# Attention and FFN block on one core: separate waits for each turned half, each v tile and each half of q and k; scores by precision pass; rk on GpSimd

## The reference

```
xn = (x - mean) / sqrt(var + 1e-5)
q, k, v = xn @ wq, xn @ wk, xn @ wv        # 8 heads of 128
q, k = rope(q), rope(k)
s = q @ k^T / 128, causal mask             # per batch and head, 512 x 512
o = softmax(s) @ v
attn = sum over heads of o @ wo
h = s0 * ([xn, -xn] @ sign(k0)); h = 2 * relu(h)      # 1024 wide
h = s1 * (h @ sign(k1));         h = 2 * relu(h)      # 1024 wide
ffn = s2 * (h @ sign(k2))
out = x + attn + ffn
```

## Time and profile before

| what | us |
|---|---|
| median of 3 runs (1779.66 to 1780.92) | 1779.78 |
| the profiled execution, its own time | 1781.45 |
| its span from first to last instruction | 1779.6 |
| TensorE, VectorE busy in the span | 1723.5, 1535.5 |

### The profile page before, as it was taken

One profiled execution on the slowest core, in us unless ns is written; L12 is line 12 of the kernel. 1 busy time (PEld: TensorE's weight loads), 2 busy tenths in 40 slices (PEclk: granted clock), 3 DMA queues, 4 the chain that ended last, 5 costly groups with the idle time before them and its releaser, 6 DMA issues.

```text
span 1779.6 us, 34027 instructions
## 1 busy us (share of the span) xinstructions
PE 1723.5 (97%) x12720; PEld 1196.4 (67%) x12720; DVE 1535.5 (86%) x3628; ACT 1269.1 (71%) x2715; POOL 923.6 (52%) x952
## 2 busy tenths in 40 slices
PE   6899989999999999999999999999999999999998
PEld 2456757767676676767767677676766767677667
DVE  8899888897988979898897988979889798888974
ACT  6777676777867678676776867778676776767773
POOL 6555544554545555455455545545455554555542
PEclk9999999999999999999999999999999999999999
DMA  5234543344343434334244433443533343343433
GB/s 171 48 55 72 94 68 78 66 82 80 55 96 63 80 66 72 78 66 96 56 87 73 66 78 66 84 78 55 96 66 78 66 72 82 63 95 59 80 65 66
DMA packets 454838, 134.08 MB, mean 75 GB/s; under 512 B 434704, under 2 KB 453648, under 8 KB 454672
## 3 DMA queue, kind: packets, MB, share of 16 engines
q1 hardware_dynamic: 454672, 131.90, 39.8%
HBM read 14.94 MB, written 8.39 MB: 13 GB/s over the span
## 4 chain that ended last, share of the span: by engine, by line
PE 67%; DVE 18%; DMA 4%; ACT 4%; POOL 3%; issue 3%; SPq 0%; DVEq 0%; POOLq 0%
PE bank L484 67%; DMA pt<-ph 3%; DVE ph L696 3%; DVE p L659 2%; DVE bank L618 2%; DVE bank L610 2%; DVE qk L628 2%; ACT p L673 2%; DVE rt L834 1%; DMA xT<-rt 1%; POOL tb L614 1%; POOL xT L316 1%; DVE v L538 1%; DVE hb L815 1%; DVE o L538 1%
## 5 line engine op out<-in xcount | busy, mean ns | idle before, releaser
L690 POOL TENSOR_SCALAR ph<-p,ri 128x384 f16<-128x384 f32 (+3 forms) x512 | 311.7, 609 | 453.5 <-DVE rk L680 416.2
L614 POOL TENSOR_TENSOR tb<-tb,sin 128x512 f32<-128x512 f32 x256 | 331.6, 1296 | 250.8 <-ACT tb L606 245.2
L484 PE MATMUL bank<-hb,wa 128*128 128x256 f16 x3360 | 379.7, 273 | 0.0
L484 PEld LDWEIGHTS bank<-hb,wa 128*128 128x128 fp8e5 x3360 | 328.0, 98 | 41.3
L673 ACT ACTIVATE p<-p,nm,sc 128x512 f32<-128x512 f32 (+3 forms) x512 | 328.6, 645 | 1.6
L696 DVE SCALAR_TENSOR_TENSOR ph<-p,rk,ph 128x512 f16<-128x512 f32 (+3 forms) x512 | 311.8, 616 | 0.0
L659 DVE CUSTOM_DVE_ANT_0 p<-bank,mask 128x512 f32<-128x512 f32 (+3 forms) x512 | 229.2, 485 | 51.1 <-PE bank L484 48.0
L484 PE MATMUL bank<-pt,v 128*128 128x256 f16 (+1 forms) x2304 | 234.0, 256 | 16.1 <-DMA pt<-ph 15.8
L484 PE MATMUL bank<-qk 128*128 128x512 f16 (+3 forms) x1536 | 231.4, 300 | 16.3 <-DVE qk L628 14.0
L484 PEld LDWEIGHTS bank<-pt,v 128*128 128x128 f16 x2304 | 203.3, 98 | 44.3 <-DMA pt<-ph 22.9
L484 PEld LDWEIGHTS bank<-qk 128*128 128x128 f16 x1536 | 133.3, 98 | 123.0 <-DVE qk L628 22.4
(11 more groups left out here) (107 smaller groups left out, 2265.5 us busy)
## 6 DMA issues: line engine op xcount, KB each, us to landing
out<-xnat SPq DMA_DIRECT2D x32, 256.0 KB, 2.3
xnat<-in_x SPq DMA_DIRECT2D x15, 512.0 KB, 3.9
pt<-ph SPq DMA_TRANSPOSE x256, 4.3
o<-in_k SPq DMA_DIRECT2D x1, 1024.0 KB, 7.8
v<-in_wq SPq DMA_DIRECT2D x1, 1024.0 KB, 9.8
v<-in_wk SPq DMA_DIRECT2D x1, 1024.0 KB, 11.6
ph<-in_wv SPq DMA_DIRECT2D x1, 1024.0 KB, 14.0
o<-in_wo SPq DMA_DIRECT2D x1, 1024.0 KB, 10.8
```

The lines of the kernel that those rows point to most:

```text
L484: self.todo.append(lambda e, stop=False: e.matmul(self.ps[:, cols[0]:cols[1]], lhsT, rhs, start=first, stop=stop, skip_group_check=skip))
L614: done["crossed", n] = pool.put(lambda e: e.tensor_tensor(tb, tb, SIN[:], ALU.mult))
L690: done["P_hi", g, i] = pool.put(lambda e: e.tensor_scalar(part(r, i, HI), v, RI[:, g % 4, i:i + 1], 4096.0, ALU.mult, ALU.mult))
```

## The change

- `s_pt` becomes a semaphore for each buffer and each q. `turned(q)` waits only for its own P_lo and issues its own transfer. The one for q = 1 has the due time `turned`, the one for q = 0 the new `turned_0`.
- `high(i)` waits for the transfer of its own q of two heads before. `values` waits, run by run, for the transfer that the run reads and for v's tile j.
- `scores` takes its three banks at once. It runs HI by HI over all four tiles, then q LO by k HI, then q HI by k LO, and waits before each pass for the halves that it reads. The fills end in the last pass.
- RK is computed on GpSimd ahead of the first P_hi, not on VectorE after RI.
- The tables `PLACES`, `SETUP`, `FIRST`, `EARLY`, `DELAY` and `HELD` have other values.

```
-    "v0": ((-3, 5), (-3, 1), (-1, 0), (0, 4)),
-    "v1": ((3, 5), (4, 1), (4, 0), (1, 4)),
+    "v0": ((-3, 5), (-3, 0), (-1, 0), (0, 4)),
+    "v1": ((3, 5), (3, 4), (4, 0), (1, 4)),
...
-FIRST = ("am0", "l1", "p0", "l1", "qk", "qk", "qk", "am2", "l1", "qk", "p2", "l1", "S", "qk", "S", "l1", "qk", "l1",
-         "v", "v", "v", "v")
+FIRST = ("l1", "am0", "p0", "l1", "qk", "qk", "qk", "am2", "qk", "l1", "p2", "l1", "S", "l1", "qk", "S", "v", "qk",
+         "v", "l1", "v", "v")
...
-EARLY = dict(qhi=(24.5, 21.1, 27.7), qlo=(23.9, 22.6, 17.8), bias=(7.0, 7.5, 7.4), exp=(6.1, 0.6, 5.3),
-             inv=(14.8, 0, 11.4), high=(3.5, 14.3, 15.5), low=(20.6, 36.1, 25.0), turned=(47.2, 23.9, 36.4),
-             rotated=(13.8, 15.3, 11.9))
+EARLY = dict(qhi=(24.1, 21.1, 27.7), qlo=(23.9, 21.8, 17.8), bias=(7.0, 8.5, 7.4), exp=(6.1, 0.6, 2.0),
+             inv=(15.6, 11.1, 11.4), high=(4.9, 14.3, 14.5), low=(21.5, 36.1, 25.0), turned=(46.2, 22.9, 30.8),
+             rotated=(13.8, 15.3, 9.8), turned_0=(52.5, 30, 37.2))
...
-DELAY = dict(hi=0, lo=11.3, swap=0, straight=9.6, crossed=0, rotated=15.5, qhi=21.8, qhi_w=0, qlo=19.8, bias=8.1,
-             exp=11.6, exp_i=1.4, differ=4.7, keep_hi=0, keep_lo=17.4, t_hi=10.6, t_lo=18.1, add=7, inv=23.5,
-             high=22.6, high_i=6.1, low=43.7, low_i=8.3, turned=66.6, x_hi=48.8, x_lo=60.5, x_turned=70.7)
+DELAY = dict(hi=0, lo=11.6, swap=0, straight=9.6, crossed=0, rotated=15.5, qhi=21.8, qhi_w=0, qlo=18.7, bias=8.1,
+             exp=11.6, exp_i=1.4, differ=5, keep_hi=0, keep_lo=16.1, t_hi=9.6, t_lo=18.1, add=7.2, inv=23.5, high=26,
+             high_i=7.9, low=43.7, low_i=8.3, turned=67.4, turned_0=76, x_hi=44.2, x_lo=55.9, x_turned=76.8)
...
-HELD = dict(am=0, p2=23.2, T=30.9, qk=30.5, S=8.2, PV=23.0, v=13.7, l0=25.3, l1=18.3, seg=21.5, l2=18.6, proj=8.7)
+HELD = dict(am=0, p2=18.0, T=22.8, qk=28.8, S=6.4, PV=23.7, v=24.5, l0=24.9, l1=18.3, seg=25.1, l2=17.6, proj=1.3)
...
-        s_pt = [sem("s_pt0"), sem("s_pt1")]
+        s_pt = [[sem(f"s_pt{r}{q}") for q in range(2)] for r in range(2)]
...
         def scores(g):
             r = g % 2
-            pe.wait(*[need(("qk_lo", 2 * g + w)) for w in range(2)])
-            for u, tiles in enumerate(S_FILLS):
-                f = Fill(("S", g, u))
-                at_col = 0
-                spans = []
-                for i in tiles:
-                    w = WIDTH[i]
-                    f.group((at_col, at_col + w),
-                            three(lambda s: QK[:, r, s, i * 128:i * 128 + 128], lambda s: QK[:, r, 2 + s, 0:w]))
-                    spans.append((i, at_col))
-                    at_col += w
-                f.end([("max", g, tiles[-1])])
+            fs = [Fill(("S", g, u)) for u in range(3)]
+            for a, c in ((HI, HI), (LO, HI), (HI, LO)):
+                for f, tiles in zip(fs, S_FILLS):
+                    at_col = 0
+                    for i in tiles:
+                        w = WIDTH[i]
+                        f.wait(need(("qk_lo" if a == LO else "qk_hi", 2 * g)),
+                               need(("qk_lo" if c == LO else "qk_hi", 2 * g + 1)))
+                        f.mm((at_col, at_col + w), QK[:, r, a, i * 128:i * 128 + 128], QK[:, r, 2 + c, 0:w],
+                             skip=len(tiles) > 1)
+                        at_col += w
+                    if c == HI:
+                        f.begin()
+                    else:
+                        f.end([("max", g, tiles[-1])])
+            for f, tiles in zip(fs, S_FILLS):
+                spans = [(i, sum(WIDTH[j] for j in tiles[:n])) for n, i in enumerate(tiles)]
...
-                dve.wait(done["inv", g])
-                done["inv_k", g] = dve.put(lambda e: e.tensor_scalar(RK[:, g % 4, :], RI[:, g % 4, :], 4096.0, None,
-                                                                     ALU.mult))
...
             def high(i):
-                pool.wait(need(("inv_k", g)))
+                pool.wait(need(("inv", g)))
+                if i == 3:
+                    done["inv_k", g] = pool.put(lambda e: e.tensor_scalar(RK[:, g % 4, :], RI[:, g % 4, :], 4096.0, None,
+                                                                          ALU.mult))
...
-                    pool.wait(need(("pt", g - 2)))
+                    pool.wait(need(("pt", g - 2, SQUARE[i][0])))
...
             def low(i):
-                dve.wait(need(("P_hi", g, i)))
+                dve.wait(need(("P_hi", g, i)), done["inv_k", g])
...
-            def turned():
-                sp.wait(*[need(("P_lo", g, i)) for i in range(4)], need("pad"))
+            def turned(q):
+                sp.wait(*[need(("P_lo", g, i)) for i in SQUARE if SQUARE[i][0] == q], need("pad"))
...
-                for q in range(2):
-                    a, n = SQ_AT[q], 2 * SQ_SIZE[q]
-                    done["pt", g] = sp.dma(lambda e, a=a, n=n: e.dma_start_transpose(
-                        PT[:, r, a // 128:(a + n) // 128, :], PH[:, r, a:a + n]), s_pt[r], 32 * (g // 2) + 16 * q + 16)
+                a, n = SQ_AT[q], 2 * SQ_SIZE[q]
+                done["pt", g, q] = sp.dma(lambda e: e.dma_start_transpose(
+                    PT[:, r, a // 128:(a + n) // 128, :], PH[:, r, a:a + n]), s_pt[r][q], 16 * (g // 2) + 16)
...
-            at(delay("turned", g), turned)
+            at(delay("turned_0", g), lambda: turned(0))
+            at(delay("turned", g), lambda: turned(1))
...
         def values(g):
-            pe.wait(need(("pt", g)))
-            pe.wait(*[need(("vp", b, h // 4, t, LO)) for t in range(4)])
             f = Fill(("PV", g))
             for j, q, i0, i1 in PV_RUNS:
+                f.wait(need(("pt", g, q)), need(("vp", b, h // 4, j, LO)))
```

More of the change, by code:

```diff
@@ L69 @@
     "l0": ((-2, 4), (0, 2), (0, 5), (1, 1)),
[4 rows of a table removed]
[4 rows of a table added]
     "seg": ((2, 2), (2, 3), (3, 2), (3, 3), (3, 3), (4, 0), (4, 2), (5, 4)),
     "seg_15": ((2, 0), (3, 4), (4, 1), (4, 2), (5, 2), (5, 2), (5, 5), (6, 5)),
-    "l2_0": ((2, 3), (4, 4)),
+    "l2_0": ((2, 3), (3, 3)),
     "l2": ((6, 3), (8, 3)),
-    "l2_15": ((8, 0), (7, 0)),
+    "l2_15": ((8, 0), (7, 3)),
     "proj": ((9, 0), (9, 3)),
 }
-SETUP = dict(v_max=93.8, o_max=60.2, a11=48.4, a12=45.7, a22=74.9, s1a=1.1, s1b=15.8, s2a=4.9, s2b=14.7, s3a=4.9,
-             s3b=1.2, s4a=76.1, s4b=91.9, k2=63.2, x1=129.9, wq1=86.9, wk1=108.5, wq2=90.5, wk2=116.1, wq3=111.9,
-             wk3=131.4, wv0=118.9, wv1=82.5, pads=117.2, ascale=168.2, wo0=147.5, wo1=161.6)
@@ L86 @@
-FIRST = ("am0", "l1", "p0", "l1", "qk", "qk", "qk", "am2", "l1", "qk", "p2", "l1", "S", "qk", "S", "l1", "qk", "l1",
-         "v", "v", "v", "v")
-EARLY = dict(qhi=(24.5, 21.1, 27.7), qlo=(23.9, 22.6, 17.8), bias=(7.0, 7.5, 7.4), exp=(6.1, 0.6, 5.3),
-             inv=(14.8, 0, 11.4), high=(3.5, 14.3, 15.5), low=(20.6, 36.1, 25.0), turned=(47.2, 23.9, 36.4),
-             rotated=(13.8, 15.3, 11.9))
+SETUP = dict(v_max=95.2, o_max=56.7, a11=56.6, a12=48.1, a22=75.7, s1a=1.3, s1b=19, s2a=11.1, s2b=14.9, s3a=1.6,
+             s3b=7.6, s4a=76.5, s4b=103.9, k2=64.5, x1=129.9, wq1=86.5, wk1=108.7, wq2=89.5, wk2=112.1, wq3=109.7,
+             wk3=131.8, wv0=120.9, wv1=79.2, pads=98.6, ascale=169.1, wo0=149.7, wo1=158.1)
```

## The result

The changed kernel takes 1814.63 us in the median (1813.58 to 1815.51, 4 runs) against 1780.26 of the kernel before: the ratio is 1.0197, 95% interval 1.0182 to 1.0211. It is slower by 34 us, where the forecast was 9 us faster. The profiled execution has a span of 1812.6 us.

What follows compares the result with a forecast made beforehand. The prediction took TensorE as the bound, its waits set by VectorE's order. Scores -10.0, start -4.0 and PV +5.0 gave -9.0 us; from the profiled 1781.45, less 1.67 to the median, that made 1770.8 us, range 1764 to 1777.

Steps and rivals of the forecast that it cites:

- a bank's reader in front of the scores: Sign that the forecast is wrong: a new TensorE wait entry over 5 us for a bank's reader before the scores.
- The shifted places and setup times: Tables: the new values move work by at most a slot and change no count; 0, within 3 us either way.
- All three banks are asked for before the first score matmul: Scores: the third bank is asked for 1.2 us earlier than before; costed at nothing, as other releasers' waits are small.
- Rival (b): Scores find low halves ready but wait for three free banks instead, losing the 10.0 us: 1780.8 us; chance 0.15.
- Eight banks with the oldest one taken: Banks: the cover named for asking for all three score banks early, at no cost.
- There is nothing left to wait for: Scores: with low halves waited for one by one, each is ready when needed; 10.0 us gained, or none.
- rival (d): Time gained at the scores is lost at the next PV, whose 20 waits grow by 0.55: 1786.8 us; chance 0.12.
- Start (-4.0): Second head's scores near 57.76 us: an l1 fill between covers the 4.03 us wait; 4.0 us gained, bounds 0 and 5.5.
- That only eats from a later wait: Start: l1 ahead of am0 leaves p0 less cover, but only shortens the later wait for the two largest values.
- Transfers (+0.45 each): PV: the long transposing transfer, issued second, lands 0.1 to 0.65 us later; each of 20 waits grows by 0.45 us.
- -0.2 each: PV: rk moved from VectorE to GpSimd shortens each of 20 PV waits by 0.2 us; VectorE loses 22.9 us.
- rival (c): GpSimd and VectorE hinder each other: each rk holds a P_lo for 0.5 us, PV waits grow: 1784.8 us; chance 0.06.

Runs made afterwards that it cites:

- s_only: The kernel before with the changed scores alone (three banks at once, high halves first, maxima due after the whole set): 1804.0 us, ratio 1.0140.
- s_lazy: s_only, but each of the three banks is asked for just before its first matmul, old tables: 1803.0 us, ratio 1.0138.
- halves: q_long with scores bank after bank, in each HI by HI first, then q's LO, then k's LO, each waited for by itself: 1763.8 us, ratio 0.9907.
- q_long: The kernel before with separate waits for transfers and v tiles, the long transfer first on its own two P_lo: 1772.1 us, ratio 0.9957.
- q_short: The kernel before with separate waits for transfers and v tiles alone, the short transfer first, old tables: 1779.3 us, ratio 1.0000.
- r_only: The kernel before with rk on GpSimd alone: 1778.9 us, ratio 0.9996.

## Why the prediction was wrong

The forecast was 1770.8 us, within 1764 to 1777, and 1814.63 was measured; the rivals, from 1756 to 1786.8, do not reach it either. Of the signs named ahead, the one of a bank's reader in front of the scores came (15.8 us behind L819), and qk L628 stayed at 17.7 us in all, not under 2.

1. **"The shifted places and setup times move work by at most a slot and change no count: 0, within 3 us either way."** This step failed, and it carries most of the error of 44 us: 29 of them, each of the two pieces measured by itself on the changed kernel. One v tile was worth 8 us, since it stood between the norm and the first reader of xT; the prediction looked for a count and not for who needs the time that the tile took. Six due times were worth 21 us. The text read DELAY only for the order of the transfers. The tables without the rest cost 47 us.
2. **"All three banks are asked for before the first score matmul ... I cost it at nothing."** Wrong in size and place. Rival (b) named the resource, at 10 us in front of the scores; s_only shows 34.7 us in front of the k products and v tiles, and s_lazy that asking early is not what costs. "Eight banks with the oldest one taken" was no cover, for the oldest is chosen by planned times. In the changed kernel the new HELD has taken these waits away, and those behind L819 (15.8 us) only take the place of waits for low halves: with the old scores it is as slow.
3. **"There is nothing left to wait for" at the scores (-10.0).** Right as a mechanism: the qk L628 waits in front of the scores fell to 4.0 us in the changed kernel and, kept in one bank, the step is worth 8.3 us (halves against q_long). The time saved was not kept in the changed kernel, as rival (d) feared, though (d)'s price and its way (PV) were wrong: PV waits fell from 15.8 to 12.7 us.
4. **Start (-4.0).** The 4.03 us wait went, but others grew by twice as much: the 9th head's PV comes 4.0 us later, an error of 8 us. "That only eats from a later wait" was wrong: the first power's wait grew from 0.40 to 2.72 us, and the later one for the largest value fell only from 3.72 to 2.88. The second power's wait (1.12 to 5.54 us) was not seen. An l1 fill is 8192 columns and a score set 3840, so it is the work of two such sets and not of five; the cover of over 3 us is right.
5. **Transfers (+0.45 each).** The order of landing was right, the size not: 0 with the old tables, and PV waits of 12.7 us in the changed kernel where about 20 were expected. The term leaned to an issue of 1.84 us, the median over both kinds; a short one in front takes 1.23. At the median both have landed 5.7 us after the first start (q_short), where it was 5.5. That long first would pay was right, and it is what the change leaves out: it took away all 20 PV waits, 0.8 us each on average, for 7.5 us of the kernel.
6. **rk (-0.2 each, rival (c)).** -1 us measured for -4, not clear of noise. VectorE's busy time did not fall by 23 us but rose by 13, and not through rk, which alone lowers it by 14.3 (1521.2 us in r_only). The rule cited there, that a GpSimd instruction and a VectorE one with two SBUF inputs exclude each other (the Trainium skill, SBUF — State Buffer, "SBUF: two separate sides"), fits the rows at 384.01 and 387.98, roughly: the P_lo from 387.98 ends 0.55 us after L614 does, and alone it takes 0.74. It speaks of every GpSimd instruction that reads SBUF, so it should have been held against the due times of DELAY, not against rk alone.

## What to carry to other kernels

Where an order is made from due times, a change of the tables is a change of every engine's queue: cost it by what stands between a producer and its first reader, and by what lands beside what, not by counts. When a step holds its banks longer, the choice of banks has to be set again, and the waits turn up in front of other work. Waiting for operands one by one paid where no more buffers were open for it: here 8 us with one bank, while with two the kernel was 2 to 3 us slower than without, and with three 24 us slower than the kernel before (s_only), under the old HELD each time.

## What the runs showed of the hardware that was not expected

P_lo, with two inputs in SBUF, takes 0.74 us for 512 columns alone, and 1.70 beside the sine product of GpSimd, which has two SBUF inputs too (387.98). The issue of the short transposing transfer takes 1.23 us when it comes first (q_short); in the kernel before, with the long one first, no issue was under 1.30 and the median was 1.84.
